# The last batch of a conditioning layer: its share of the routing, the rows' transfers and TensorE's order rewritten

## The reference, cut to what matters

```
x = x + L0_ffn(L0_cond(x))          # per-batch adapter, 8 experts that choose tokens
x = x + L1_ffn(L1_cond(x))          # below

# L1_cond: gates, eight causal decays, a projection and a LayerNorm -> z
# L1_ffn on z (4096 tokens, 256 channels), 64 experts, 8 per token:
logits = z @ router_w.T;  probs = softmax(logits)
topk_w, topk_ids = top_k(probs, 8);  topk_w /= sum(topk_w)
pos    = position of the token in its expert's list (first 128 are kept)
y      = (silu(xb @ w_gate) * (xb @ w_up)) @ w_down        # per expert, 128 rows
routed = sum over the token's experts of topk_w * y
shared = (silu(z @ ws_gate) * (z @ ws_up)) @ ws_down       # every token
result = routed + shared
```

## Time and profile before

| | |
|---|---|
| three executions | 1119.07, 1118.03, 1116.71 us |
| the profiled execution | 1117.48 us, span 1115.7 us, mean granted TensorE clock 0.933 |
| TensorE / VectorE / ScalarE / GpSimd busy | 951.7 / 745.3 / 460.7 / 664.6 us |
| last batch's share (step 9) | about 834 to 863 us |
| expert stage, from the first gather to the last scatter | 859.0 to 1091 us |
| last transfer, `odd_rows` added to `out` | issued at 1091.2 us, 23.2 us to landing |

### The profile page before, as it was taken

One profiled execution on the slowest core, in us unless ns is written; L12 is line 12 of the kernel. 1 busy time (PEld: TensorE's weight loads), 2 busy tenths in 40 slices (PEclk: granted clock), 3 DMA queues, 4 the chain that ended last, 5 costly groups with the idle time before them and its releaser, 6 DMA issues. The chain is left out here.

```text
span 1115.7 us, 14812 instructions
## 1 busy us (share of the span) xinstructions
PE 951.7 (85%) x4524; PEld 665.8 (60%) x4524; DVE 745.3 (67%) x1522; ACT 460.7 (41%) x835; POOL 664.6 (60%) x496
## 2 busy tenths in 40 slices
PE   4969999999999999987379889987687899988960
PEld 2433698899989998862145454444454565555640
DVE  3657566667666766524779999999855787767610
ACT  1330444554455545533455666566320232222320
POOL 2112344555455544407999999999831577777870
PEclk9989999999999999998689999999786899999995
DMA  5879234444354432223223642325078599996558
GB/s 176 284 231 347 58 76 118 90 87 99 76 122 89 93 87 39 30 85 75 95 70 103 221 157 80 117 97 184 23 216 281 152 271 266 259 251 143 90 76 155
DMA packets 94006, 155.46 MB, mean 139 GB/s; under 512 B 16296, under 2 KB 74352, under 8 KB 90800
## 3 DMA queue, kind: packets, MB, share of 16 engines
q1 hardware_dynamic: 52336, 91.27, 25.1%
q0 software_dynamic: 25104, 39.86, 20.3%
q10 hardware_dynamic: 16496, 23.49, 6.2%
HBM read 119.56 MB, written 43.42 MB: 146 GB/s over the span
## 5 line engine op out<-in xcount | busy, mean ns | idle before, releaser
L641 POOL TENSOR_TENSOR wide<-wide 128x1024 f32<-128x1024 f32 x64 | 156.4, 2458 | 32.0 <-issue 32.0
L1278 DVE TENSOR_TENSOR_SCAN wide<-bank,wide 128x512 f32<-128x512 f32 x128 | 149.3, 1208 | 21.7 <-POOL wide L641 21.6
L878 ACT ACTIVATE h_raw<-bank,b 128x512 f32<-128x512 f32 x128 | 88.0, 688 | 168.3 <-PE bank L1642 165.9
L1215 DVE TENSOR_TENSOR h_lo<-h_raw,h_hi 128x512 fp32r<-128x512 f32 x128 | 87.2, 692 | 93.1 <-ACT h_hi L882 93.1
L1657 PE MATMUL bank<-w_hi,h_hi 128*128 128x256 f32 x512 | 144.4, 282 | 0.1
L1657 PE MATMUL bank<-w_lo,h_hi 128*128 128x256 f32 x512 | 142.2, 278 | 0.0
L1657 PE MATMUL bank<-w_hi,h_lo 128*128 128x256 f32 x512 | 142.1, 278 | 0.0
L615 POOL DMA_INDIRECT x_rows<-ob,put x64 | 110.1, 1721 | 28.3 <-issue 16.0
L649 POOL TENSOR_TENSOR wide<-wide 128x1024 f32<-128x1024 f32 x46 | 108.4, 2356 | 11.9 <-issue 8.1
L902 ACT ACTIVATE wide<-wide,blend 128x512 f32<-128x512 f32 x128 | 84.1, 715 | 62.0 <-POOL wide L641 58.4
L1642 PE MATMUL bank<-ex_hi,w_hi 128*128 128x512 f32 x256 | 100.3, 392 | 2.5 <-issue 2.5
(11 more groups left out here) (239 smaller groups left out, 1999.6 us busy)
## 6 DMA issues: line engine op xcount, KB each, us to landing
wide<-in_mwp SPq DMA_DIRECT2D x40, 512.0 KB, 4.3
wide<-m_rows SPq DMA_DIRECT2D x16, 1024.0 KB, 4.7
w1s<-in_fW SPq DMA_DIRECT2D x8, 1024.0 KB, 5.1
w2s<-in_fW SPq DMA_DIRECT2D x8, 1024.0 KB, 5.2
own<-in_mwp SPq DMA_DIRECT2D x15, 512.0 KB, 4.2
head<-in_mwp SPq DMA_DIRECT2D x9, 512.0 KB, 4.3
xT<-in_xT ACTq DMA_DIRECT2D x8, 512.0 KB, 4.2
xt<-in_x ACTq DMA_DIRECT2D x8, 512.0 KB, 6.8
```

The costliest lines, as they stand in the source:

```text
L641: G.tensor_tensor(drive[n % DRIVES], gb[d % 2], md[d // HD][:, d % HD, :].unsqueeze(1).to_broadcast([P, CT, S]), ALU.mult).then_inc(c_u, 1)
L878: A.activation(h1_raw[f % 4][:, :], bank[:, 2 + f % 4, :], ACT.Gelu_apprx_tanh, bias=b1_0[:, bass.ds(e, 1), f]).then_inc(b_h, 1)
L1215: V.tensor_tensor(h1_lo[:, f, :], h1_raw[f % 4][:, :], h1_hi[:, f, :].bitcast(F32), ALU.subtract).then_inc(b_lo, 1)
L1278: o = V.tensor_tensor_scan(dst[:, c, :], decay[:, d:d + 1].to_broadcast([P, S]), drive[(D * b + d) % DRIVES][:, c, :], 0.0, ALU.mult, ALU.add)
```

## The change

The conditioning steps up to b = 8 stay as they are, except for one `turn`. For the last batch:

- **Transfers.** The two transfers of batch 7's `zrow` leave SyncE's queue and go to GpSimd's own: `last_rows(slice(0, H))` in step 9 after the rows are normalised, and `last_rows(slice(H, ZW))` once `c_zr` says that the weights are written. Both count on a new semaphore `z_last`, on which the first gather waits.
- **Slots.** On VectorE group 0 comes before the shared expert, and so do the parts of group 1 up to part 2, mixed with the shared expert's two multiplications; part 3 of group 1 stands between the row scalings of experts 0 and 1.
- **Shared expert.** `shared_a_in` is cut into its up half and its gate half. In the last batch the up half runs early, the gate half after `shared_b`; `down_in(B - 1)` moves into the expert loop behind expert 0's `gate_up`, and `finish(B - 1)` behind expert 1's scaling. The last batch uses other PSUM banks (4, 5 and 6, 7), and `hidden_in(0)` waits for `finish`.
- **TensorE.** Six calls of `turn` are added, ten `turn` products in all.

```diff
+        def act_banks(q):
+            return (4, 5) if q == B - 1 else (2, 3)
+        def down_bank(q):
+            return 6 if q == B - 1 else 4
...
-                if on(b - 2):
+                if on(b - 2) and b < B + 1:
                     z_store(b - 2)
...
-                if on(b - 2) and b != B:
+                if on(b - 2) and b < B:
                     weight_store(b - 2)
...
+            def last_rows(part):
+                pool.dma_start(z_rows[(B - 1) * S:TOK, part].rearrange("(t p) c -> p t c", p=P), zrow[:, :, part]).then_inc(z_last, 16)
...
             def step(b):
                 if on(b - 2):
                     rstd_of(b - 2)
+                if b == B + 1:
+                    pool.wait_ge(c_no, level(B - 1, TT))
+                    last_rows(slice(0, H))
...
-            pool.wait_ge(c_zst, level(B - 1, 16))
-            pool.wait_ge(c_zwt, level(B - 1, 16))
+            pool.wait_ge(c_zst, level(B - 2, 16))
+            pool.wait_ge(c_zwt, level(B - 2, 16))
+            pool.wait_ge(c_zr, level(B - 1))
+            last_rows(slice(H, ZW))
+            wait_moved(pool, z_last, 1, 16)
...
             def last_share():                      # VectorE
 
                 pick(B - 1)
-                shared_b(B - 1)
                 prep(0, 1)
                 route_weights(B - 1)
                 prep(0, 2)
-                shared_a(B - 1)
                 prep(0, 3)
                 prep(1, 0)
-                finish(B - 1)
+                shared_b(B - 1)
                 prep(1, 1)
+                prep(1, 2)
+                shared_a(B - 1)
                 dve.drain()
...
             xgT_out(0)
+            prep(1, 3)
             xgT_out(1)
-            prep(1, 2)
+            finish(B - 1)
...
                 if e == 0:
-                    prep(1, 3)
-                    dve.drain()
                     prep(2, 0)
...
+            def shared_a_up(q):
+                for c in range(CT):
+                    T.matmul(bank[:, act_banks(q)[1], :], ws_gu[:, c, 2 * P:3 * P], zT[:, c, :], ...)
+            def shared_a_gate(q):
+                pe.wait_ge(c_hsB, level(q))
+                for c in range(CT):
+                    o = T.matmul(bank[:, act_banks(q)[0], :], ws_gu[:, c, 0:P], zT[:, c, :], ...)
+                o.then_inc(c_am, 1)
...
             def down_in(q):
...
-                pe.wait_ge(c_fin, level(q - 1))
+                if q == B - 1:
+                    pe.wait_ge(e_slot, level(0))
+                else:
+                    pe.wait_ge(c_fin, level(q - 1))
...
             def drain_share():                     # TensorE
...
                 down_in(B - 2)
+                turn(6, 2)
                 z_in(B - 1)
 
             def last_share():                      # TensorE
+                turn(1, 2)
                 logits_in(B - 1)
                 shared_b_in(B - 1)
+                turn(1, 2)
                 prep(0, 0)
-                shared_a_in(B - 1, 0)
+                shared_a_up(B - 1)
                 prep(0, 1)
-                shared_a_in(B - 1, 1)
+                turn(1, 1)
                 prep(0, 2)
-                down_in(B - 1)
+                turn(0, 2)
                 prep(1, 0)
                 prep(1, 1)
+                shared_a_gate(B - 1)
+                turn(0, 1)
+                prep(1, 2)
...
-            pe.wait_ge(c_fin, level(B - 1))
+            pe.wait_ge(c_fin, level(B - 2))
...
             def hidden_in(e):
                 pe.wait_ge(e_h, level(e))
                 pe.wait_ge(e_ys, level(e - 2))
+                if e == 0:
+                    pe.wait_ge(c_fin, level(B - 1))
...
                 if e == 0:
+                    down_in(B - 1)
                     rows_in(1)
...
-                if e == 0:
-                    prep(1, 2)
```

More of the change, by code:

```diff
@@ L334, in build @@
         c_xr, c_zst, c_ost = sem("c_xr", 16), sem("c_zst", 16), sem("c_ost", 16)
-        c_zwt = sem("c_zwt", 16)
+        c_zwt, z_last = sem("c_zwt", 16), sem("z_last", 0)
         (c_Tm, c_x1T, c_ctx, c_wgm, c_wgt, c_gat, c_h1m, c_h1, c_som, c_so, c_u,
@@ L974, in shared_out @@
                 act.wait_ge(c_am, level(q))
-                A.activation(sgA[:, :], bank[:, 2, :], ACT.Tanh, scale=0.5).then_inc(c_at, 1)
+                A.activation(sgA[:, :], bank[:, act_banks(q)[0], :], ACT.Tanh, scale=0.5).then_inc(c_at, 1)
             def step(b):
@@ L1356, in shared_a @@
                 dve.wait_ge(c_at, level(q))
-                V.scalar_tensor_tensor(hsA[:, :], sgA[:, :], 1.0, bank[:, 2, :], ALU.add, ALU.mult)
+                V.scalar_tensor_tensor(hsA[:, :], sgA[:, :], 1.0, bank[:, act_banks(q)[0], :], ALU.add, ALU.mult)
                 dve.drain()
-                V.tensor_tensor(hsA[:, :], hsA[:, :], bank[:, 3, :], ALU.mult).then_inc(c_hsA, 1)
+                V.tensor_tensor(hsA[:, :], hsA[:, :], bank[:, act_banks(q)[1], :], ALU.mult).then_inc(c_hsA, 1)
             def route_weights(q):
@@ L1376, in finish @@
                 dve.wait_ge(c_ost, level(q - 1, 16))
-                V.scalar_tensor_tensor(ost[:, :, :], rows4(4), 0.5, xr[:, :, :], ALU.mult, ALU.add).then_inc(c_fin, 1)
+                V.scalar_tensor_tensor(ost[:, :, :], rows4(down_bank(q)), 0.5, xr[:, :, :], ALU.mult, ALU.add).then_inc(c_fin, 1)
             def prep(k, part):
@@ L1748, in shared_b_in, with shared_a_in @@
                 o.then_inc(c_bm, 1)
-            def shared_a_in(q, half=None):
-                if half != 1:
-                    pe.wait_ge(c_hsB, level(q))
-                for n, lo in ((0, 0), (1, 2 * P)):
-                    if half in (None, n):
-                        for c in range(CT):
-                            o = T.matmul(bank[:, 2 + n, :], ws_gu[:, c, lo:lo + P], zT[:, c, :], start=(c == 0),
-                                         stop=(c == CT - 1))
-                if half != 0:
-                    o.then_inc(c_am, 1)
+            def shared_a_up(q):
+                for c in range(CT):
+                    T.matmul(bank[:, act_banks(q)[1], :], ws_gu[:, c, 2 * P:3 * P], zT[:, c, :], start=(c == 0), stop=(c == CT - 1))
+            def shared_a_gate(q):
+                pe.wait_ge(c_hsB, level(q))
+                for c in range(CT):
+                    o = T.matmul(bank[:, act_banks(q)[0], :], ws_gu[:, c, 0:P], zT[:, c, :], start=(c == 0), stop=(c == CT - 1))
+                o.then_inc(c_am, 1)
+            def shared_a_in(q):
+                shared_a_up(q)
+                shared_a_gate(q)
             def down_in(q):
@@ L1767, in down_in @@
                     pe.wait_ge(c_pad, 1)
-                pe.wait_ge(c_fin, level(q - 1))
+                if q == B - 1:
+                    pe.wait_ge(e_slot, level(0))
+                else:
+                    pe.wait_ge(c_fin, level(q - 1))
+                into = rows4(down_bank(q))
                 for j in range(TT):
-                    T.matmul(rows4(4)[:, j, :], hsA[:, j * P:(j + 1) * P], ws_da[:, :], start=True, stop=False)
-                    o = T.matmul(rows4(4)[:, j, :], hsB[:, j * P:(j + 1) * P], ws_db[:, :], start=False, stop=True)
+                    T.matmul(into[:, j, :], hsA[:, j * P:(j + 1) * P], ws_da[:, :], start=True, stop=False)
+                    o = T.matmul(into[:, j, :], hsB[:, j * P:(j + 1) * P], ws_db[:, :], start=False, stop=True)
                 o.then_inc(c_dm, 1)
```

## The result

The changed kernel's first eight executions had a median of 1109.93 us (1108.36 to 1111.76), the kernel before beside them 1117.88: ratio 0.9921, 95 % interval 0.9897 to 0.9945. That is 8.8 us faster by the ratio, 8.0 by the two medians. Twelve later executions of the same kernel gave 1112.40 us beside 1117.63, and a ratio of 0.9961 (0.9939 to 0.9982): 4.4 us by the ratio, 2.0 to 6.8 by its interval. All twenty against 132 of the kernel before (one of 1168 us left out): 1111.8 against 1118.45 us on the mean, 6.7 +- 1.4 us faster, with an interval that counts all executions alike and leaves out that the two sets differ. The direction was forecast.

The account below looks back on a forecast made before the run. Bounds: the weights' store, then group 1's slots, with TensorE's clock third. Expert 3's start 4.8 us earlier, less 0.7 for half clock, gave 4.1: 1113.4 profiled, median 1113.7; own range 1112.0 to 1115.6, with rivals 1, 2, 3, 5 1111.2 to 1117.3.

Parts of the forecast that it names:

- The fills and the logits: Last batch on TensorE: fills ahead of the logits cost 0.2 us; shared b product takes 1.8 instead of 3.73.
- The transfers: Weights' store on GpSimd's queue, issued 845.7, lands in 9 us at 854.7; first gather 855.6, 3.4 us earlier.
- rival 1: Weights' store lands early, in 5 us; `shared_a` on VectorE then bounds; gain 0.9 us more, 1112.8; chance 0.15.
- Slots of group 0 and 1: Last batch's slots: group 0 at 851.3, 5.3 us earlier; group 1 at 863.0, ending the fifth gather's wait.
- Half clock: TensorE idles in pieces from 850.5 to 853.9; gate half and fill partly at 1.2 GHz, taking 0.7 us off.
- Up to expert 3: Start of the expert loop, product down on the path: `gate_up(3)` at 872.8 instead of 877.58, 4.8 us.
- The stage behind: The 60 more experts, released by the experts' own progress, all shift as one, keeping the gain to the end.
- rival 3: Transfers pace the expert stage from 900 to 1010 us, taking back half of 4.1 us: 1115.6; chance 0.09.
- Rivals 2, 4 and 5: Landing no earlier, 1116.4 (0.12); fills at half clock, 1120.5 (0.08); fills not holding the clock from 834, 1116.0 (0.08).
- The sum: Whole kernel: 1117.48 - 4.1 = 1113.4 us for the profiled execution, median 1113.7; chance 0.48.

Follow-up runs that it names:

- x1: Changed kernel with all its fill products (six `turn` calls) taken out; ratio to the kernel before 0.9956 (0.9935 to 0.9977).
- x10: Changed kernel with only the four fills ahead of the transposes and the logits, the six behind out; ratio 0.9961 (0.9937 to 0.9985).
- x9: Changed kernel timed and profiled again, nothing altered; 1112.40 us, ratio 0.9961 (0.9939 to 0.9982).
- x8: Changed kernel with the last batch's two stores on ScalarE's queue instead of GpSimd's; ratio 0.9946 (0.9925 to 0.9968).
- x2: Changed kernel with both stores of the last batch back on SyncE's queue, order and fills kept; ratio 0.9999 (0.9973 to 1.0025).
- x16: Changed kernel, two fills in group 1's gap, none behind gate half, two behind expert 0's transposes, last four loads late; 1108.47 us, ratio 0.9925.
- x7: Changed kernel with two fills between group 1's first and second slot products, none behind the gate half; ratio 0.9940 (0.9915 to 0.9966).
- x12: Changed kernel with two fills in group 1's gap, none behind the gate half, and step 8's last four loads late; ratio 0.9938 (0.9916 to 0.9960).
- x17: Kernel before, profiled again, nothing altered; expert 3's `gate_up` 46.6 us after the mark, rest of the span 239.1 us; no ratio given.
- x18: Kernel before, profiled a third time, nothing altered; expert 3's `gate_up` 47.4 us after the mark, rest of the span 239.7 us; no ratio given.
- x14: Changed kernel without the loads of experts 24 to 63, computing them with weights left in the ring; median 1098.57 us.
- x15: Kernel before without the loads of experts 24 to 63, computing them with weights left in the ring; median 1109.52 us.
- x6: Changed kernel with both stores on SyncE's queue and step 8's 16 expert loads issued behind the weights' store; 1117.28 us, ratio 0.9982.
- x4: Kernel before with only six of the ten fill products added; ratio 1.0022 (0.9993 to 1.0051).

## Why the prediction was wrong

**The fills and the logits: this step failed.** It said "I count 0.2 us" for the logits and kept their 3.67 us. The earlier trace rows show the clock at 0.5 in front of the logits, the logits behind it, and I re-timed the shared product for the clock, not the logits. They took 1.98. Instead of 0.2 us late VectorE started 1.6 early, and everything down to the slots came 2.0 us earlier than forecast: weights written at 12.7 us after the mark (forecast 14.7), slots of group 0 at 18.2 (20.4). x1 and x10 show that it is the fills that do it.

**The transfers: mechanism right, size off.** 9 us taken, 6.5 measured (5.9 in x9); with the earlier issue the first gather came at 20.0 instead of 24.7. The store was still the last to arrive, by 1.5 us, not 3.4. The gather itself was sized too small: it met the loads and took 5.0 us to land (6.7 in x9), not the 3.0 to 3.2 of the sum; its cover at the transposes was 1.7 us (0.7 in x9). The landing was near rival 1's, and as rival 1 said the gather then left the path; at 26.7 TensorE's own order was the bound, where rival 1 had VectorE's `shared_a`. x8 shows that a first gather 2.5 us later still would have cost nothing. x2 shows what it would have cost to leave the store behind the loads: 6.3 of the 7.2 us of the share, and all of the time.

**Slots of group 0 and 1: right.** The durations were as read; group 1's slots were at 30.8 (forecast 32.1), and the fifth gather no longer waited in the chain that counts.

**Half clock: right, and under-priced.** The gate half took 3.8 us (forecast 3.7), and the third slot product came at 26.2 (forecast 28.7, from 859.6). I took only 0.7 us for it, because the late gather would have covered the rest; with the gather early nothing did. In x16, with the clock at 1.0 throughout, `gate_up(0)` and expert 3 come 2.2 us earlier; x16 also has the last four loads late, so the 2.2 are not the clock's alone. What I had not seen either is that with the gate half at full clock the fall can move to `gate_up(0)` and the product down (x7, x12).

**Up to expert 3.** From `gate_up(0)` to `gate_up(3)` I counted 12.6 us, it took 11.35; the product down took 3.6 as forecast. Up to `gate_up(2)` it was 8.45 instead of 9.2, and the last step 2.9 instead of 3.4.

**The stage behind: not contradicted.** "All shifts as one" holds to 0.1 us in the two first profiles. That is partly luck, for the stage is 3.6 us longer in x9 than in the changed kernel's first profile, and up to 1.5 us longer in x17 and x18 than in the first profile of before. x14 and x15 agree to 0.2 us, but they take away the full transfer engines on which rival 3 rests, so they don't test it. Against rival 3 stand the times: 6.7 +- 1.4 us gained at the end of some 7.4 gained in the share, where half would be 3.7; the second set alone (2.0 to 6.8 us) doesn't exclude that. x6 shows a case near rival 3's. Rivals 2, 4 and 5 did not occur: the clock stayed 1.0 over the first four fills in both profiles of the changed kernel.

**The sum.** Expert 3's `gate_up` was forecast at 42.6 us after the mark with the 0.7, measured 39.5: 3.1 us, of which 1.85 had been gained at `gate_up(0)` and 1.25 on the way from expert 0 to 3. The 1.85 are in the main the logits' clock: x10, with the logits at full clock, has `gate_up(0)` 1.65 us earlier than x1, without. The early landing adds nothing (x8). What makes the 1.25 was not tested. Had the terms been sized so, the forecast's 4.1 would have been 7.2. The recorded median lies 1.3 us below the range; the second set's median, 1112.40, lies in it, and its interval contains 4.1. The pooled 6.7 +- 1.4 us excludes 4.1. So the profiles, not the times, carry the verdict on the step. The range held the mechanism's errors and left nothing for the scatter of sets of executions, which was as large: 4.4 us between the ratios of the two.

**Open.** Whether anything of the 6.7 us comes before the mark: the kernel before (with x15) had it at 830.9 to 834.1 in four profiles, all others at 825.3 to 833.9. No run tells that from scatter. In x4 and x15 expert 3 stood at 51.0 and 49.5 us; which pause set the clock there was not tested.

## What to carry to other kernels

Where the clock's level changes along a chain, re-time every product behind the point of change, the narrow ones too; a fall is paid by all that follows until it is back. Parts that each remove one of several waits in a row are worth little alone (here 1.6 us as a sum of their ratios, -2.9 of their shares) and more in one (7 us of the share): price them by the last wait that remains. Measure a moved stretch from an unchanged event just ahead of it; here that repeated to 0.01 us in the changed kernel and to 0.8 in the kernel before, where whole executions differed by 10.

## What the runs showed of the hardware

A transfer of 128 KB in 512 pieces (512 rows of 256 bytes) lands, beside full transfer engines, 10.1 to 11.0 us after its issue on the queue of the loads (seven profiles), 8.9 on ScalarE's (x8 alone), 5.7 to 6.5 on GpSimd's, and 2.0 with nothing beside it (x6). A gather of 128 rows took 5.0 and 6.7 us beside the end of the loads (changed kernel, x9), and 3.0 behind them (x2). Products of 64 columns with a load of 128 columns each took 0.12 us (1.98 / 16) at full clock and 0.23 at half, so they halved their pace with the clock as the wide ones did. In x7 and x12 the granted clock fell from 2.4 to 1.2 GHz (1.0 to 0.50 in the rows) after TensorE had stood for 1.9 us in front of expert 0's work. In x4 it stood idle from 849.3 us and the clock was 1.00 up to 853, so the length of a pause alone didn't say here when the fall came.
